# Attention q and k: six stacked copies stored, or three parts stored once and stacked by the loads

## The chip, the cores and the metric

The kernel runs on one core of one Trainium2 chip. The metric is the device time of one execution in microseconds (us); several executions are timed and their median is given. A profile is one further execution, recorded by the hardware profiler.

## The reference

A network of sixteen layers over x of 4 x 1024 tokens with 128 channels: attentions, feed-forward layers, state-space layers. Every layer adds its output to x. Five of them (2, 4, 6, 8 and 14) are causal attentions with 16 heads; cut to what matters, as layer 4 has it:

```python
def proj(w, b):
    y = jnp.einsum('bsd,ed->bse', x, w) + b
    return y.reshape(B, S, N_HEADS, HEAD_DIM).transpose(0, 2, 1, 3)
q = rope(proj(wq, bq))
k = rope(proj(wk, bk))
v = proj(wv, bv)
score = jnp.einsum('bhqd,bhkd->bhqk', q, k) / math.sqrt(HEAD_DIM)
score = jnp.where(causal[None, None], score, -jnp.inf)
attn = jax.nn.softmax(score, axis=-1)
out = jnp.einsum('bhqk,bhkd->bhqd', attn, v)
```

Layers 4 and 6 have rope (a rotation of channel pairs by position), layer 2 weights the probabilities by a decay instead, layer 8 has biases and no rope, layer 14 has heads of 4 channels and a bias by distance (alibi). The others have heads of 8 channels.

## The kernel before, in words

x stays in SBUF as 128 channels x 4096 tokens. Each attention is a layer norm, a projection stage (`attn_project`) and a core stage (`attn_core`); between stages all engines meet at a barrier.

**Projection.** The tokens are taken in eight halves of 512, two per batch element (here: batch). For q and for k TensorE multiplies, VectorE writes the value to t1 (with rope three operations), and three bf16 parts are made: ScalarE casts the value to the high part, GpSimd subtracts, ScalarE casts the rest to the middle part, and VectorE (plain layers) or GpSimd (rope) subtracts again for the low part. hi, mid and low count 16 of these each, four per batch. The parts lie in the SBUF tensor `part`, 128 channel rows (64 in layer 14).

A score product in near-f32 precision is six products of parts, `PAIRS`. They are summed in the contraction of one matmul: a head's q has 6 slots of dq rows, slot s holding part PAIRS[s][0], and its k the same with PAIRS[s][1]. SyncE (L506 to L518) waits for a batch's parts and stores the six q slots to DRAM, each a transfer of 128 rows of 1024 tokens; ScalarE stores the six k slots between its casts (`store_k`, L616). After batch 0's twelve stores have landed, SyncE loads stacks 0, 1 and 2. The stage ends when all stores have landed.

**A stack** is four heads: two (i) in partitions 0 and 64 onwards, two (p) side by side in the row. `load_stack` (L438) fills it by four transfers of 48 rows x 2 pieces of 1024, and two small ones of zero rows; layer 14 adds two of alibi rows. Three buffers take turns. Rows r0 to r0 + 2 of q hold the negated row maxima, in three parts as well.

**Core.** Sixteen groups, one per stack. In group n TensorE works through a string `PLAN` of a (scores for the row maxima, of the stack ahead), b (scores for the exponential, of stack n) and v (values). VectorE reduces the a scores (L1046); unit a number 14 of a group (16 in layer 2) is the first to read stack n + 2, and waits for its load (`stack_in`). SyncE's order in group n is: the maxima's rows of stack n + 1 (`max_rows`, L746), then, when all b scores of stack n are done, the load of stack n + 3, then every fourth group a step of the batch that is finished (`sums_back` L761, `inverse_rows` L765, `heads_back` L768), then the group's output and sums (L752, L754).

```python
if n + 1 < GROUPS:
    max_rows(n + 1)
if n + 3 < GROUPS:
    sp.wait_ge(b_ready, 4 * NS_ * (n + 1))
    load_stack(sp, n + 3)
...
if n >= 4 and n % 4 == 0:
    sums_back(n // 4 - 1, HEADS)
```

Of the kernel before, what the change touches and what calls it, by code (L numbers as in the profile page):

```python
# [10 lines left out]
BF16 = mybir.dt.bfloat16  # L11
# [5 lines left out]
P = 128  # L17
# [386 lines left out]
PAIRS = ((0, 0), (0, 1), (0, 2), (1, 0), (1, 1), (2, 0))  # L404
# [12 lines left out]
def attention(net, tag, w, dq, scale, rope=False, alibi=False, decay=False, bias=False, out_bias=False):  # L417
# [4 lines left out]
    parts = {n: nc.dram_tensor(f"{tag}_{n}_rows", (B * HEADS * 6 * dq, S), BF16, kind="Internal").ap() for n in "qk"}  # L422
# [3 lines left out]
    with stage(nc, tag) as (sb, ps, sem):  # L426
# [11 lines left out]
        def load_stack(sp, n):  # L438
            u = n % 3
            for n_, dst in (("q", qs[u]), ("k", ks[u])):  # L440
                src = parts[n_][n * 24 * dq:(n + 1) * 24 * dq, :].rearrange("(p i r) t -> i r p t", p=2, i=2)
                for i in range(2):
                    sp.dma_start(dst[64 * i:64 * i + 6 * dq, :, :], src[i]).then_inc(stack_in[u], 16)
# [28 lines left out]
def attn_project(net, tag, w, dq, rope, bias, decay, parts, v, qs, ks, load_stack, load_consts_):  # L472
# [4 lines left out]
    with stage(nc, tag + "_proj") as (sb, ps, sem):  # L477
# [22 lines left out]
        with nc.Block() as block:  # L500
            @block.sync
            def _(sp):
# [3 lines left out]
                for b in range(B):  # L506
                    sp.wait_ge(hi, 4 * (b + 1))
                    sp.wait_ge(mid, 4 * (b + 1))
                    sp.wait_ge(low, 4 * (b + 1))
                    for slot in range(6):  # L510
                        sp.dma_start(parts["q"].rearrange("(b h s d) t -> b s h d t", b=B, s=6, d=dq)[b, slot],
                                     part[0:R, 0, PAIRS[slot][0], b * S:(b + 1) * S]
                                     ).then_inc(stored if b else first_stored, 16)
                    if b == 0:
                        sp.wait_ge(first_stored, 16 * 12)
                        for n in range(3):
                            load_stack(sp, n)
# [84 lines left out]
            def _(act):  # L602
# [13 lines left out]
                def store_k(b):  # L616
                    act.wait_ge(low, 4 * b + 4)
                    for slot in range(6):
                        act.dma_start(parts["k"].rearrange("(b h s d) t -> b s h d t", b=B, s=6, d=dq)[b, slot],
                                      part[0:R, 1, PAIRS[slot][1], b * S:(b + 1) * S]  # L620
                                      ).then_inc(stored if b else first_stored, 16)
# [44 lines left out]
def attn_core(net, tag, w, dq, r0, scale, alibi, decay, out_bias, v, qs, ks, heads_out, sums, rsums, consts, c_in,  # L666
# [36 lines left out]
    with stage(nc, tag + "_core") as (sb, ps, sem):  # L703
# [2042 lines left out]
```

## Time and profile before

| | |
|---|---|
| median of 3 runs | 5800.48 us (5797.83 to 5809.48) |
| the profiled execution's own time | 5776.4 us |
| its span, first to last instruction | 5774.7 us |
| busy: TensorE, VectorE, ScalarE, GpSimd | 4735.2, 3787.2, 3161.8, 1684.7 us |
| mean granted TensorE clock | 0.919 of full speed |
| moved by DMA | 239.83 MB in 146884 packets |

The span is cut into instructions with start, length and what ended the idle time before them. Engines: PE is TensorE, DVE VectorE, ACT ScalarE, POOL GpSimd, SP SyncE; a q behind the name (SPq, ACTq) marks the issuing of a transfer, whose length is the time that the engine's queue is held. A packet is one contiguous piece that a DMA engine moves. A window's row gives the stretch, its length, the busy time (and count) of PE, PEld, DVE, ACT and POOL, the granted clock, the mean busy share of the 16 DMA engines and GB/s. "l_" in a name stands for any layer.

### The profile page before, as it was taken

The numbers are of one execution on the slowest core, as the hardware profiler recorded it, in microseconds if no ns is written. First come the engines' busy times: TensorE is split into PE (matmuls) and PEld (weight loads), VectorE is DVE, ScalarE is ACT, GpSimd is POOL, SyncE is SP. The second block draws the span as 40 slices with busy tenths as digits, with TensorE's granted clock in tenths as the row PEclk, the third lists the DMA queues.
The fourth block names the chain that finished last, engine by engine and source line by source line (L and its number), as shares of the span: only waits on it lengthen the run. The fifth ranks groups of instructions, "written<-read, shape, count | busy, mean of one in ns | idle before, by whom it ended". The sixth has DMA issues, their size and how long they took to land. (4 is left out here: it accounts for less than half of the span.)

```text
span 5774.7 us, 90836 instructions
## 1 busy us (share of the span) xinstructions
PE 4735.2 (82%) x33596; PEld 2081.6 (36%) x33596; DVE 3787.2 (66%) x4596; ACT 3161.8 (55%) x6002; POOL 1684.7 (29%) x1468
## 2 busy tenths in 40 slices
PE   5677667998569977699776998589867799699999
PEld 2233224443223336233352333256422344233344
DVE  6899658886579943799437992677539710699410
ACT  5655444766438853388534885444466421388621
POOL 0666315886032225323152220000006400222100
PEclk8899888999779989799897999789989999799999
DMA  0000012221032225322253220000000000211100
GB/s 27 0 1 1 4 49 76 44 44 29 10 112 42 55 65 177 115 51 51 74 154 120 50 46 20 6 10 2 5 10 0 20 0 0 60 31 45 42 0 15
DMA packets 146884, 239.83 MB, mean 42 GB/s; under 512 B 37382, under 2 KB 66930, under 8 KB 145076
## 3 DMA queue, kind: packets, MB, share of 16 engines
q1 hardware_dynamic: 125748, 197.74, 12.8%
q10 hardware_dynamic: 15744, 28.32, 1.5%
q0 software_dynamic: 4992, 8.41, 0.6%
q8 instruction: 254, 4.16, 0.3%
q14 instruction: 146, 1.20, 0.1%
HBM read 153.93 MB, written 80.31 MB: 41 GB/s over the span
## 5 line engine op out<-in xcount | busy, mean ns | idle before, releaser
L946 ACT ACTIVATE l_core_probs<-l_core_ps_scores_b 128x512 f32<-128x512 f32 (+3 forms) x3840 | 1611.3, 510 | 570.7 <-PE l_core_ps_scores_b L862 415.6
L1046 DVE TENSOR_REDUCE l_core_chunk_max<-l_core_ps_scores_a 128x2 f32<-128x1024 f32 (+3 forms) x1280 | 1253.3, 1020 | 83.9 <-PE l_core_ps_scores_a L847 48.6
L862 PE MATMUL l_core_ps_scores_b<-l_q_rows_sb,l_k_rows_sb 64*128 64x512 bf16 (+3 forms) x3840 | 944.5, 333 | 32.2 <-ACT l_core_probs L946 9.7
L847 PE MATMUL l_core_ps_scores_a<-l_k_rows_sb,l_q_rows_sb 64*128 64x512 bf16 (+3 forms) x3840 | 740.2, 346 | 121.1 <-DVE l_core_chunk_max L1046 44.7
L995 POOL TENSOR_SCALAR_AFFINE_SELECT l_core_probs<-l_core_probs 128x512 f32<-128x512 f32 x512 | 325.4, 636 | 1161.4 <-ACT l_core_probs L946 1156.4
L877 PE MATMUL l_core_ps_acc<-l_core_probs,l_v 128*9 128x512 f32 (+3 forms) x6144 | 647.7, 494 | 16.0 <-ACT l_core_out_sums L928 9.0
L862 PEld LDWEIGHTS l_core_ps_scores_b<-l_q_rows_sb,l_k_rows_sb 64*128 64x128 bf16 x3840 | 304.0, 94 | 690.0 <-ACT l_core_probs L946 607.9
L1046 DVE TENSOR_REDUCE l_core_neg_max<-l_core_ps_scores_a 128x2 f32<-128x256 f32 (+3 forms) x640 | 493.4, 819 | 84.8 <-PE l_core_ps_scores_a L807 83.0
L1917 POOL TENSOR_TENSOR l_scan_bx<-l_xs,l_scan_b_rows 128x1024 f32<-128x1024 f32 x192 | 452.3, 2356 | 224.2 <-DVE l_scan_states L1927 217.8
L1927 DVE TENSOR_TENSOR_SCAN l_scan_states<-l_scan_ps_decay,l_scan_bx 128x1024 f32<-128x1024 f32 x192 | 439.7, 2290 | 40.8 <-POOL l_scan_bx L1917 15.3
L965 POOL TENSOR_TENSOR l_core_probs_decayed<-l_core_probs,l_decay 128x1536 f32<-128x1536 f32 (+2 forms) x160 | 394.0, 2487 | 142.9 <-ACT l_core_probs L946 142.9
L807 PE MATMUL l_core_ps_scores_a<-l_mask_q_rows,l_identity_halves 64*128 64x128 bf16 (+1 forms) x5120 | 402.9, 211 | 0.0
L1862 PE MATMUL l_scan_ps_y<-l_scan_states_c,ident 128*128 128x512 f32 x768 | 362.5, 595 | 0.0
L1890 ACT ACTIVATE l_scan_ps_decay<-l_delta,l_a_cols 128x1024 f32<-128x1024 f32 x192 | 214.6, 1118 | 253.3 <-DVE l_scan_states L1927 253.3
L847 PEld LDWEIGHTS l_core_ps_scores_a<-l_k_rows_sb,l_q_rows_sb 64*128 64x128 bf16 x3840 | 204.0, 94 | 371.8 <-DVE l_core_chunk_max L1046 174.6
L807 PEld LDWEIGHTS l_core_ps_scores_a<-l_mask_q_rows,l_identity_halves 64*128 64x128 bf16 x5120 | 305.5, 98 | 79.0 <-issue 15.3
L1561 DVE SCALAR_TENSOR_TENSOR x_res<-l_ps_out,l_scales,x_res 128x512 f32 x16 | 12.0, 751 | 486.9 <-PE l_ps_out L1534 486.9
L1550 ACT ACTIVATE l_gelu<-l_ps_hidden,l_scales 128x512 f32<-128x512 f32 x128 | 87.9, 687 | 384.7 <-PE l_ps_hidden L1522 384.7
L1812 POOL TENSOR_TENSOR l_xs<-l_xs,l_delta x16 | 28.9, 1805 | 776.3 <-DVE l_delta L1802 776.3
L1852 PE MATMUL l_scan_ps_c_rows<-l_bc_parts,l_spread 128*128 128x512 bf16 x384 | 117.9, 389 | 148.2 <-DVE l_scan_states_c L1935 148.2
L638 POOL MEMSET l_q_rows_sb<- 128x2048 bf16 x5 | 9.0, 1804 | 764.8 <-POOLq L49 764.8
L1935 DVE TENSOR_TENSOR l_scan_states_c<-l_scan_states,l_scan_ps_c_rows 128x1024 f32<-128x1024 f32 x192 | 229.4, 1195 | 1.4 <-PE l_scan_ps_c_rows L1852 1.4
(323 smaller groups left out, 7711.9 us busy)
## 6 DMA issues: line engine op xcount, KB each, us to landing
l_slots_weights<-m_both_dram SPq DMA_DIRECT2D x78, 512.0 KB, 4.7
l_k_rows<-l_proj_parts ACTq DMA_DIRECT2D x96, 256.0 KB, 5.3
l_q_rows<-l_proj_parts SPq DMA_DIRECT2D x96, 256.0 KB, 5.1
l_q_rows_sb<-l_q_rows SPq DMA_DIRECT2D x128, 192.0 KB
l_k_rows_sb<-l_k_rows SPq DMA_DIRECT2D x128, 192.0 KB
l_heads_out<-l_core_out_sums SPq DMA_DIRECT2D x300, 32.0 KB
l_core_heads<-l_heads_out SPq DMA_DIRECT2D x15, 512.0 KB, 5.6
l_core_inverse_rows<-l_rsums SPq DMA_DIRECT2D x15, 512.0 KB, 7.0
```

What stands on the lines that cost most here:

```text
L807: mm = nc.tensor.matmul(dst[:, cols[h]], eye[rows, h, :], mask[rows, h, cols[h]], start=False, stop=(h == 1))
L847: mm = nc.tensor.matmul(slot[:, i, 0:w], qs[n % 3][rows, p, qt * P:(qt + 1) * P], ks[n % 3][rows, p, c * NT:c * NT + w], start=True, stop= ...
L862: mm = nc.tensor.matmul(pb[m % 3][:, 0:w], ks[n % 3][rows, p, kt * P:(kt + 1) * P], qs[n % 3][rows, p, q0:q0 + w], start=True, stop=not diag)
L877: mm = nc.tensor.matmul(acc[32 * j:32 * j + 9, NT - w:NT], ones9[:, :] if decay else v[:, n, kt, j, :], pt[:, ts % RP, j, 0:w], start=(kt ...
L946: nc.scalar.activation(pt[:, ts % RP, j, 0:w], pb[m % 3][:, 0:w], ACT.Exp, scale=scale).then_inc(b_free, 1)
L965: nc.gpsimd.tensor_tensor(pw[:, had_decay(ts) % RW, :, 0:wd], pt[:, ts % RP, :, 0:wd], dtab[:, :, off:off + wd].to_broadcast((P, 4, wd)), ...
L995: nc.gpsimd.affine_select(block_, block_, [[0, 4], [1, P]], ALU.is_ge, none, base=0, channel_multiplier=-1).then_inc(cut, 1)
L1046: nc.vector.tensor_reduce(to, pa[e % 2][:, :, 0:width_a(qt, c)], AX.X, ALU.max, negate=True).then_inc(a_free, 1)
L1862: mm = nc.tensor.matmul(acc[:, c * NT:(c + 1) * NT], net.ident[:, :], hc[:, q % R, c * NT:(c + 1) * NT], start=(n == 0), stop=(n == NS - 1))
L1917: nc.gpsimd.tensor_tensor(bx[:, q % R, :], xs[:, h, b * S:(b + 1) * S], bs[:, q % RS, :], ALU.mult).then_inc(bx_done, 1)
L1927: nc.vector.tensor_tensor_scan(hs[:, q % RS, :], pa[:, :], bx[:, q % R, :], 0.0, ALU.mult, ALU.add).then_inc(scanned, 1)
L1935: nc.vector.tensor_tensor(hc[:, q % R, :], hs[:, q % RS, :], pc[:, :], ALU.mult).then_inc(hc_done, 1)
```

## The change

DRAM holds each of the three parts of q and of k once. SyncE stores them, all six, after every half of a batch, in transfers of 128 rows of 512 tokens; ScalarE stores nothing. `load_stack` puts the six slots together: `RUNS` lists runs of slots that share one part of q (a broadcast source) and take successive parts of k. The host permutes the columns of the q and k weights, biases and rope tables so that the rows which lie side by side in a stack are neighbours in DRAM; it costs the device nothing. Stack 0 is loaded after batch 1's stores, stack 1 after batch 2's, stack 2 at the start of the core. `sums_back` stands ahead of the load of a stack.

```diff
-PAIRS = ((0, 0), (0, 1), (0, 2), (1, 0), (1, 1), (2, 0))
+RUNS = ((0, 0, 0, 3), (3, 1, 0, 2), (5, 2, 0, 1))
...
-    parts = {n: nc.dram_tensor(f"{tag}_{n}_rows", (B * HEADS * 6 * dq, S), BF16, kind="Internal").ap() for n in "qk"}
+    parts = {n: nc.dram_tensor(f"{tag}_{n}_rows", (3, B * HEADS * dq, S), BF16, kind="Internal").ap() for n in "qk"}
...
-            for n_, dst in (("q", qs[u]), ("k", ks[u])):
-                src = parts[n_][n * 24 * dq:(n + 1) * 24 * dq, :].rearrange("(p i r) t -> i r p t", p=2, i=2)
-                for i in range(2):
-                    sp.dma_start(dst[64 * i:64 * i + 6 * dq, :, :], src[i]).then_inc(stack_in[u], 16)
+            for i in range(2):
+                lines = slice(n * 4 * dq + i * 2 * dq, n * 4 * dq + (i + 1) * 2 * dq)
+                for at, part, first, slots in RUNS:
+                    rows = slice(64 * i + at * dq, 64 * i + (at + slots) * dq)
+                    src = parts["q"][part, lines, :].rearrange("(o d p) t -> o d (p t)", o=1, p=2)
+                    sp.dma_start(qs[u][rows, :, :].rearrange("r p t -> r (p t)"),
+                                 src.to_broadcast((slots, dq, 2 * S))).then_inc(stack_in[u], 16)
+                    src = parts["k"][first:first + slots, lines, :].rearrange("s (d p) t -> s d (p t)", p=2)
+                    sp.dma_start(ks[u][rows, :, :].rearrange("r p t -> r (p t)"), src).then_inc(stack_in[u], 16)
...
-                    for slot in range(6):
-                        sp.dma_start(parts["q"].rearrange("(b h s d) t -> b s h d t", b=B, s=6, d=dq)[b, slot],
-                                     part[0:R, 0, PAIRS[slot][0], b * S:(b + 1) * S]
-                                     ).then_inc(stored if b else first_stored, 16)
-                    if b == 0:
+                    for h in range(2):
+                        sp.wait_ge(hi, 4 * b + 2 * h + 2)
+                        sp.wait_ge(mid, 4 * b + 2 * h + 2)
+                        sp.wait_ge(low, 4 * b + 2 * h + 2)
+                        for j, n in enumerate("qk"):
+                            for s_ in range(3):
+                                sp.dma_start(parts[n][s_, b * R:(b + 1) * R, h * NT:(h + 1) * NT],
+                                             part[0:R, j, s_, b * S + h * NT:b * S + (h + 1) * NT]
+                                             ).then_inc(stored if b else first_stored, 16)
+                    if b == 1:
                         sp.wait_ge(first_stored, 16 * 12)
-                        for n in range(3):
-                            load_stack(sp, n)
+                    if b in (1, 2):
+                        load_stack(sp, b - 1)
...
-                def store_k(b):
...
-        NST = 16 * (6 + (2 if alibi else 0))
+        NST = 16 * (14 + (2 if alibi else 0))
...
+                load_stack(sp, 2)
                 max_rows(0)
                 for n in range(GROUPS):
                     if n + 1 < GROUPS:
                         max_rows(n + 1)
+                    if n >= 4 and n % 4 == 0:
+                        sums_back(n // 4 - 1, HEADS)
                     if n + 3 < GROUPS:
                         sp.wait_ge(b_ready, 4 * NS_ * (n + 1))
                         load_stack(sp, n + 3)
...
-                    if n >= 4 and n % 4 == 0:
-                        sums_back(n // 4 - 1, HEADS)
```

How the order on the engines moves. SyncE's queue in the projection of layer 2, before: the q stores of batch 0, three stacks, the q stores of batches 1 to 3 (l_q_rows and l_k_rows are the DRAM tensors, the same with _sb the stack buffers; the shape is that of the transfer's destination or source rows).

```order
L511 DMA l_q_rows<-l_proj_parts 16x8x1024 x6
L443 DMA l_q_rows_sb<-l_q_rows 48x2x1024 x2
L443 DMA l_k_rows_sb<-l_k_rows 48x2x1024 x2
L445 DMA l_q_rows_sb<-zero_rows_dram 3x2048 x2
L443 DMA l_q_rows_sb<-l_q_rows 48x2x1024 x2
```

The same queue now, from the last half of batch 1 to the middle of stack 0.

```order
L521 DMA l_q_rows<-l_proj_parts 128x512 x3
L521 DMA l_k_rows<-l_proj_parts 128x512 x3
L448 DMA l_q_rows_sb<-l_q_rows 24x1x2048
L451 DMA l_k_rows_sb<-l_k_rows 24x1x2048
L448 DMA l_q_rows_sb<-l_q_rows 16x1x2048
L451 DMA l_k_rows_sb<-l_k_rows 16x1x2048
L448 DMA l_q_rows_sb<-l_q_rows 8x2048
L451 DMA l_k_rows_sb<-l_k_rows 8x2048
```

A store is one transfer of 128 rows of 512; the four large loads of a stack have become twelve, of 24, 16 and 8 rows, and stores of the batches 2 and 3 stand behind one stack each.

ScalarE's queue at the end of batch 1 of layer 2, before, with the six k stores between the casts.

```order
L613 ACTIVATE l_proj_parts<-l_proj_t 128x512 x2
L607 ACTIVATE l_proj_parts<-l_proj_t 128x512 x2
L613 ACTIVATE l_proj_parts<-l_proj_t 128x512
L619 DMA l_k_rows<-l_proj_parts 16x8x1024 x6
L607 ACTIVATE l_proj_parts<-l_proj_t 128x512
```

The same place now.

```order
L623 ACTIVATE l_proj_parts<-l_proj_t 128x512 x2
L617 ACTIVATE l_proj_parts<-l_proj_t 128x512 x2
L623 ACTIVATE l_proj_parts<-l_proj_t 128x512
L617 ACTIVATE l_proj_parts<-l_proj_t 128x512
L623 ACTIVATE l_proj_parts<-l_proj_t 128x512
```

The casts follow one another, and the queue holds no transfer.

SyncE's queue in the core of layer 2 at n = 4, before.

```order
L746 DMA l_q_rows_sb<-l_core_max_parts 2x16x128 x3
L443 DMA l_q_rows_sb<-l_q_rows 48x2x1024 x2
L443 DMA l_k_rows_sb<-l_k_rows 48x2x1024 x2
L445 DMA l_q_rows_sb<-zero_rows_dram 3x2048 x2
L761 DMA l_core_inverse<-l_sums 128x128
```

And now.

```order
L746 DMA l_q_rows_sb<-l_core_max_parts 2x16x128 x3
L761 DMA l_core_inverse<-l_sums 128x128
L448 DMA l_q_rows_sb<-l_q_rows 24x1x2048
L451 DMA l_k_rows_sb<-l_k_rows 24x1x2048
L448 DMA l_q_rows_sb<-l_q_rows 16x1x2048
```

The fetch of the sums has moved from behind the load to ahead of it.

## Rows read from the trace of the kernel before

**Rows 1.** The page, part 1: busy time, share of the span and instructions of each engine.

```profile
PE 4735.2 (82%) x33596; PEld 2081.6 (36%) x33596; DVE 3787.2 (66%) x4596; ACT 3161.8 (55%) x6002; POOL 1684.7 (29%) x1468
```

**Rows 2.** Timeline of SyncE, layer 2's projection: start, length, engine, line, what, count.

```profile
844.14 6.92 SPq L511 DMA_DIRECT2D l_q_rows<-l_proj_parts  x6
855.20 0.82 SPq L443 DMA_DIRECT2D l_q_rows_sb<-l_q_rows  x2
866.51 21.31 SPq L511 DMA_DIRECT2D l_q_rows<-l_proj_parts  x18
```

**Rows 3.** Timeline of SyncE: a 128-row load of a weight, and alibi rows (layer 14).

```profile
808.18 0.43 SPq L137 DMA_DIRECT2D l_proj_w<-a_wk_dram  x1
...
4960.18 0.91 SPq L449 DMA_DIRECT2D l_q_rows_sb<-alibi_q_dram  x1
```

**Rows 4.** Timeline of ScalarE, layer 2's projection; in brackets the idle time before.

```profile
844.06 6.30 ACTq L619 DMA_DIRECT2D l_k_rows<-l_proj_parts  x6
850.40 0.63 ACT L607 ACTIVATE l_proj_parts<-l_proj_t 128x512 bf16<-128x512 f32 x1 [7.91 <-issue]
...
857.01 5.84 ACTq L619 DMA_DIRECT2D l_k_rows<-l_proj_parts  x6
```

**Rows 5.** Windows, first store to the core's first VectorE instruction; last: clock, DMA share, GB/s.

```profile
844.14:893.20 49.06, 24.40 (x80) 14.55 (x78) 25.58 (x54) 12.31 (x22) 13.56 (x10) 0.72 0.89 307
1612.34:1670.35 58.01, 30.48 (x100) 17.39 (x100) 32.93 (x63) 13.79 (x24) 29.19 (x24) 0.80 0.83 259
2324.53:2383.92 59.39, 30.23 (x100) 16.22 (x100) 31.42 (x64) 13.79 (x24) 29.30 (x24) 0.80 0.82 253
3034.83:3086.39 51.56, 23.50 (x79) 13.74 (x78) 25.88 (x53) 12.30 (x22) 13.56 (x10) 0.71 0.88 291
4949.21:4993.51 44.30, 21.80 (x79) 13.80 (x78) 25.46 (x54) 12.30 (x22) 13.53 (x10) 0.73 0.74 176
```

**Rows 6.** Timeline of VectorE, end of layer 2's projection and start of its core.

```profile
880.88 1.66 DVE L598 COPY l_v<-l_proj_ps_v 128x128 f32<-128x128 f32 x8
...
889.90 0.88 DVE L598 COPY l_v<-l_proj_ps_v 128x128 f32<-128x128 f32 x4 [0.16 <-PE l_proj_ps_v L532]
893.20 0.48 DVE L1004 MEMSET l_core_ps_acc<- 128x512 f32 x1 [2.42 <-PEq L49]
```

**Rows 7.** Timelines of SyncE and TensorE, layer 4's core: stack 3's load and first use.

```profile
1727.83 0.81 SPq L443 DMA_DIRECT2D l_q_rows_sb<-l_q_rows  x2
...
1743.15 0.22 PE L847 MATMUL l_core_ps_scores_a<-l_k_rows_sb,l_q_rows_sb 64*128 64x128 bf16 x2
```

**Rows 8.** Windows: 2 KB stores, 4 KB loads, 1 KB rows, a stack's load (2 KB).

```profile
846.00:849.50 3.50, 2.69 (x4) 0.50 (x2) 0.47 (x1) 0.00 (x0) 0.00 (x0) 0.67 1.03 370
1140.00:1141.00 1.00, 1.00 (x24) 0.79 (x22) 0.89 (x3) 0.89 (x4) 1.00 (x1) 1.00 1.05 389
3613.30:3614.30 1.00, 1.00 (x4) 0.50 (x3) 0.00 (x0) 0.52 (x2) 0.00 (x0) 1.00 0.56 152
984.00:989.00 5.00, 5.00 (x85) 2.38 (x82) 4.16 (x5) 3.82 (x9) 4.34 (x3) 1.00 0.81 162
```

**Rows 9.** Timeline of GpSimd, layer 4's projection.

```profile
1605.01 1.15 POOL L643 TENSOR_TENSOR l_proj_t<-l_proj_t,l_proj_parts 128x512 f32<-128x512 f32 x1 [0.33 <-ACT l_proj_parts L613]
1606.12 1.61 POOL L650 TENSOR_TENSOR l_proj_parts<-l_proj_t,l_proj_parts 128x512 f32 x1
```

**Rows 10.** DMA packets in 983:990 (stack load), 960.6:965 (output), 979:983.1 (maxima), 1399.5:1408 (heads, inverse).

```profile
DMA packets 461, 0.83 MB, mean 118 GB/s; under 512 B 70, under 2 KB 70, under 8 KB 460
...
DMA packets 74, 0.17 MB, mean 39 GB/s; under 512 B 36, under 2 KB 36, under 8 KB 72
...
DMA packets 102, 0.02 MB, mean 6 GB/s; under 512 B 102, under 2 KB 102, under 8 KB 102
...
DMA packets 192, 0.68 MB, mean 80 GB/s; under 512 B 28, under 2 KB 28, under 8 KB 191
```

**Rows 11.** Transfers by line, whole trace: a small one; last, us to landing.

```profile
l_rsums<-l_core_inverse SPq DMA_DIRECT2D x15, 64.0 KB, 2.1
```

More of the change, by code:

```diff
@@ L614, in second @@
                                          ACT.Copy).then_inc(mid, 1)
-                def store_k(b):
[L617 to L621, printed above, removed]
                 for b in range(B):
@@ L2572, in thirds, with stack_order @@
     return np.stack([hi, mid, low])
+def stack_order(dq):
+    return np.arange(HEADS * dq).reshape(4, 2, 2, dq).transpose(0, 2, 3, 1).reshape(-1)
 def shape_constants():
@@ L2582, in shape_constants @@
     freq = (1.0 / 10000.0 ** ((d // 2 * 2).astype(f) / 8)).astype(f)
-    theta = pos[None] * freq[:, None]
-    sign = np.where(d % 2 == 0, -1.0, 1.0).astype(f)[:, None]
+    order = stack_order(8)
+    theta = pos[None] * freq[order, None]
+    sign = np.where(d[order] % 2 == 0, -1.0, 1.0).astype(f)[:, None]
     rope = np.stack([np.cos(theta), np.sin(theta) * sign], 1).astype(f)
@@ L2626, in attention_layouts @@
     swap = np.arange(P) ^ 1
+    order, order4 = stack_order(8), np.tile(stack_order(4), 2)
     out = {}
     w = i["L0_attn_b_W_attn"]
-    out.update(a0_wq=w[:, :P], a0_wk=w[:, P:2 * P], a0_wv=w[:, 2 * P:], a0_wo=i["L0_attn_b_W_proj"])
+    out.update(a0_wq=w[:, :P][:, order], a0_wk=w[:, P:2 * P][:, order], a0_wv=w[:, 2 * P:], a0_wo=i["L0_attn_b_W_proj"])
     for n, wn, f in (("a1", "L1_attn_a_w", lambda m: m.T), ("b1", "L1_attn_b_W", lambda m: m)):
         q, k, bq, bk = f(i[wn + "q"]), f(i[wn + "k"]), i[wn[:-1] + "bq"], i[wn[:-1] + "bk"]
-        out.update({f"{n}_wq": q, f"{n}_wk": k, f"{n}_wv": f(i[wn + "v"]), f"{n}_wo": f(i[wn + "o"]),
-                    f"{n}_wq_sw": q[:, swap], f"{n}_wk_sw": k[:, swap], f"{n}_bq": one(bq), f"{n}_bk": one(bk),
-                    f"{n}_bq_sw": one(bq[swap]), f"{n}_bk_sw": one(bk[swap]),
+        out.update({f"{n}_wq": q[:, order], f"{n}_wk": k[:, order], f"{n}_wv": f(i[wn + "v"]), f"{n}_wo": f(i[wn + "o"]),
+                    f"{n}_wq_sw": q[:, swap[order]], f"{n}_wk_sw": k[:, swap[order]],
+                    f"{n}_bq": one(bq[order]), f"{n}_bk": one(bk[order]),
+                    f"{n}_bq_sw": one(bq[swap[order]]), f"{n}_bk_sw": one(bk[swap[order]]),
                     f"{n}_bv": row(i[wn[:-1] + "bv"]), f"{n}_bo": one(i[wn[:-1] + "bo"])})
@@ L2638, in attention_layouts @@
     for j, n in enumerate("qkv"):
-        out[f"a2_w{n}"] = w[:, :, j].reshape(D, P)
-        out[f"a2_b{n}"] = (row if n == "v" else one)(b[:, j].reshape(P))
+        cols = slice(None) if n == "v" else order
+        out[f"a2_w{n}"] = w[:, :, j].reshape(D, P)[:, cols]
+        out[f"a2_b{n}"] = (row if n == "v" else one)(b[:, j].reshape(P)[cols])
     out.update(a2_wo=i["L2_attn_a_out_W"], a2_bo=one(i["L2_attn_a_out_b"]))
-    out.update(b3_wq=np.tile(i["L3_attn_b_Wq"], (1, 2)), b3_wk=np.tile(i["L3_attn_b_Wk"], (1, 8)),
+    out.update(b3_wq=i["L3_attn_b_Wq"][:, order4], b3_wk=np.tile(i["L3_attn_b_Wk"], (1, 8))[:, order4],
                b3_wv=np.tile(i["L3_attn_b_Wv"], (1, 4)), b3_wo=i["L3_attn_b_Wp"], b3_bo=one(i["L3_attn_b_bp"]))
```

6 lines of the change are left out of this document (removed).

## The prediction

> **What bounds the kernel now.** First the page's busy times [rows 1]: no engine is busy throughout (TensorE 82% of the span), so the answer lies in stages. The edit touches the five attentions in two places: the projection stage, which writes q and k to DRAM, and the core, which reads them back as stacks.
>
> In the projection the queues of SyncE and ScalarE come first. In layer 2 SyncE takes 6.92 us to issue six q stores and 21.31 us for the other eighteen [rows 2]: 1.15 and 1.18 us each, while a plain 128-row transfer is issued in 0.43 us [rows 3]. ScalarE spends 6.30 us issuing six k stores and stands 7.91 us without a cast [rows 4]. The windows say why: from the first store to the first instruction of the core the DMA engines are 89% busy at 307 GB/s in layer 2, 82 to 88% in layers 4, 6 and 8, and 74% in layer 14, over 49.06, 58.01, 59.39, 51.56 and 44.30 us [rows 5]. The stage is nearly bound by the transfers. VectorE's last copy of v ends at 890.78 and the core begins at 893.20 [rows 6], so compute, delayed by the blocked ScalarE, ends only just before the transfers.
>
> In the core a stack's load starts when the group before has done its matmuls, 1727.83 in layer 4, and TensorE first reads that stack at 1743.15 [rows 7]: 15.3 us of room. The same distance holds in layers 6, 8 and 14; layer 2 has more. Thirteen stacks of each attention are loaded so.
>
> **The change, part by part.**
>
> *Stores.* 24 q stores on SyncE and 24 k stores on ScalarE, 256 KB each, become 48 stores of 128 KB on SyncE: the bytes halve, their 1 KB rows are as many as the 2 KB rows were. A full-rate window of 2 KB stores gives 16 x 2048 / 370 = 89 ns per row and engine, and a 1 KB one 0.56 x 16 x 1024 / 152 = 60 ns [rows 8]. The ends are 45 (half of 89) and 89 ns; I take 60, the row of that size. A store is then 8 rows on each of 16 engines, 0.48 us, and its issue 0.43 us plus a gap of some 0.04 [rows 3]. Twelve stores, a batch's worth, cost 5.7 us either way, where 12 old ones took 12 x 8 x 89 ns = 8.5 us of transfer. Issue bounds: 0.43 as here, or 1.15 as the old stores [rows 2]; I take 0.43, since the old ones were held up by the full DMA engines.
>
> *ScalarE without stores.* It loses the 6 us stalls. Its casts of a batch take 6.61 us (850.40 to 857.01) [rows 4]; in the layers with rope GpSimd sets the pace, 1.15 + 1.61 + 0.33 = 3.1 us per half of q or k, 12.3 per batch [rows 9]. Compute then ends about 20 us after the first store in the plain layers (30 with v's copies, 9.9 us from 880.88 by the same copies) and 37 us in the rope ones. That is ahead of what follows, so the casts hide behind the transfers and are costed at nothing.
>
> *Loads of a stack.* Four transfers of 192 KB become twelve: for q and for k and for each half of the partitions, runs of three, two and one slots, of 24, 16 and 8 rows of 4 KB. The bytes are the same, the engines are not. The trace tells how many engines a transfer uses, since each engine adds one packet of under 512 B to the data: four old loads and two of three rows leave 70 = 4 x 16 + 2 x 3; eight stores of 8 and 1 rows leave 36 = 4 x 8 + 4 x 1; three transfers whose destination has an outer dimension of 2 leave 102 - 96 = 6 [rows 10]. The source counts too: a load of 96 rows and one whose destination has 96 rows but whose source repeats 12 leave 28 = 16 + 12 [rows 10]. In the new loads the source's outer dimension is the slot, 3 or 2, so I forecast 3, 2 and 8 engines. The Trainium skill has this as a rule (DMA: Bandwidth & Descriptors, "Rules for kernel authors": an outermost dimension of c copies keeps the whole transfer on at most c engines), and it speaks against this edit; by that rule, the trace agrees.
>
> The first two engines then carry 8 + 8 + 1 rows, four times over: 68 rows of 4 KB per stack, 272 KB, where each of 16 carried 48 KB. A stream of 4 KB rows gives 16 x 4096 / 389 = 168 ns [rows 8], so a stack takes 11.4 us. Bounds: 68 x 120 = 8 us if twice the 1 KB price is all that 4 KB needs, and 68 x 328 = 22 us at twice the 164 ns which 2 KB rows took when 16 engines wrote 48 partitions [rows 8]. I take 168, same size and direction; with two or three engines at work there is less to collide than in that window. A layer-14 stack has half the rows: 34 and one or two more, 6.1 us, about what its sixteen issues cost, two of them 0.91 us [rows 3].
>
> *In the core.* 11.4 us plus the 2.1 us that a small transfer needs from issue to landing [rows 11] is 13.5 us, within 15.3. Costed at nothing, with 1.8 us of cover left. SyncE issues 14 instead of 6 transfers, some 5 us; the sums' stores behind them are not needed for a group's length. Moving the sums' fetch ahead of the load takes it out from behind those long transfers; its one reader, VectorE's inversion, comes within the same group after a third of its work, so it gains nothing. Stack 2 now loads at the start of the core and is needed a group and a half later: hidden. The maxima's rows of stack 0, queued behind it, exist only when all 24 of its reductions are done: hidden too.
>
> *The projection's new length.* Stacks 0 and 1 are loaded between stores, so each of the first two engines does, after batch 1's last stores: load, 12 stores, load, 12 stores = 2 x (11.4 + 5.7) = 34.2 us. Before it: batch 1's casts, 6.6 us after batch 0's (12.3 with rope), and six stores, 2.9 us. After it: 2.1 us to land and the 2.4 us between 890.78 and 893.20 [rows 6]. Together 48.2 us plain, 53.9 with rope, and 6.6 + 2.9 + 2 x (6.1 + 5.7) + 4.5 = 37.6 in layer 14. Against rows 5:
>
> - layer 2: 49.06 to 48.2, -0.9
> - layer 4: 58.01 to 53.9, -4.1
> - layer 6: 59.39 to 53.9, -5.5
> - layer 8: 51.56 to 48.2, -3.4
> - layer 14: 44.30 to 37.6, -6.7
>
> The sum is -20.6 us, 0.36%. The profiled execution took 5776.4 us, 24 below the median of the runs, 5800.5; I subtract the difference from the median: **5780 us**. What comes next as the bound in the projection is the pair of engines that load the stacks, with the other fourteen idle for two thirds of that time.
>
> **The rivals.**
>
> *A: the loads spread over more engines,* or the pair is faster than I think. Then SyncE's issue is the limit: 14 issues at 0.3 to 0.43, 5.6 us, in place of 11.4, twice, so another 11.6 us off in each of four layers and none in layer 14, where issue already counts: -67, 5734 us. For it: halved bytes, a queue that is freed of backlog. Against: the packet counts [rows 10]. 0.12.
>
> *B: slower, a stack that comes late in the core.* Its place is TensorE's first read of a stack in layers 4, 6 and 8, 13 times each. It decides from 68x + 2.1 > 15.3, x = 194 ns per row. At 220 ns, a third more than my row and well below the 328 of the bound, each stack comes 1.8 us late: 39 x 1.8 = 68 us, and each load in the projection is 3.5 us longer, 2 x 4 x 3.5 = 28. With -20.6 that is +76, 5876 us; at 205 ns it is 29 + 20 - 20.6 = +28, 5829 us. For it: rows of 164 ns per 2 KB in this very load [rows 8]. Against: these came when 16 engines wrote to a few partitions. 0.15.
>
> *C: hardly any change, SyncE alone is the bound.* If a store costs 0.6 us to issue rather than 0.47, twelve take 7.2 us: 2 x 1.5 + 0.8 = 3.8 us more in each of five layers, and the sum is -1.6: 5799 us. At 0.78 it would be about +26. For it: all 48 stores now stand in one queue behind 28 loads, with ScalarE's queue empty. The Trainium skill says that issuing from more engines saves only the sequencer's time (DMA: Bandwidth & Descriptors, "Rules for kernel authors"). 0.2.
>
> **How the numbers follow.** The forecast has 0.53: -11 to -36 us for 4 KB rows between 177 and 150 ns and stores between 0.5 and 0.43 us. A measurement of this kernel tells 0.2%, about 12 us, from no change. Faster: A whole, and four fifths of the forecast, 0.55. Slower: B, and of C the part with dearer issue, 0.15 + 0.06 = 0.21. The rest, 0.24, is within. The range leaves out half of A below (5746) and the worse half of B above (5825).
>
> **What would show it.** Right: packets under 512 B of a stack load at 3, 2 and 8 per transfer; a stack's 4 KB packets over some 11 to 12 us; no wait of TensorE for a stack; stages between 48 and 54 us; ScalarE without gaps for stores. Wrong: rows of a "DMA q_rows_sb" releaser before TensorE's score matmuls in layers 4, 6 and 8 (B); store issues above 0.55 us with idle DMA engines (C); a projection under 45 us (A). The forecast falls altogether if the core's groups change in length at all.

## The result, and the profile after

The change measures **5795.89 us** against 5804.11 us for the kernel before (21 runs each): a ratio of 0.9987, 95% interval 0.9981 to 0.9993. A second set of runs gave 0.9991 (0.9982 to 1.0000). That is 8 us less, two fifths of the 20.6 us that the prediction forecast, and within the 0.2% that it called no change. The bytes written to DRAM fell by a third (80.31 to 52.00 MB), DMA packets by a tenth, and almost nothing came of it.

The page of the kernel after, parts 1 to 3; TensorE's busy time is as in [rows 1].

```profile
PE 4718.3 (81%) x33501; PEld 2088.3 (36%) x33596; DVE 3782.7 (65%) x4596; ACT 3159.8 (55%) x6002; POOL 1685.3 (29%) x1468
...
DMA packets 132106, 211.55 MB, mean 37 GB/s; under 512 B 36422, under 2 KB 93619, under 8 KB 130293
...
HBM read 153.93 MB, written 52.00 MB: 36 GB/s over the span
```

The windows of the kernel after, from the first store to the core's first VectorE instruction, answer to [rows 5].

```profile
838.79:888.65 49.86, 21.79 (x84) 12.84 (x82) 27.71 (x57) 14.31 (x26) 15.61 (x12) 0.76 0.46 159
1603.24:1657.77 54.53, 30.42 (x107) 16.14 (x105) 37.61 (x68) 15.09 (x27) 34.74 (x27) 0.90 0.44 145
2326.83:2381.75 54.92, 31.42 (x107) 17.34 (x105) 38.21 (x69) 15.10 (x27) 34.72 (x27) 0.89 0.43 144
3049.63:3099.13 49.50, 20.89 (x83) 12.84 (x82) 27.95 (x57) 14.23 (x25) 15.55 (x12) 0.81 0.48 160
4965.35:5018.48 53.13, 21.88 (x83) 13.06 (x82) 27.37 (x57) 14.08 (x25) 15.56 (x12) 0.75 0.33 79
```

The DMA engines went from 0.74 to 0.89 busy to under half, and yet four windows lie within 1.7 us of the forecast 48.2 and 53.9; the fifth, layer 14, took 53.1 where 37.6 was forecast. A window starts at its first store, though, which now leaves after half a batch and not a whole one. So the fair measure is a whole stage, from VectorE's clearing of v's last column (L549; L539 before) to its clearing of the accumulator (L1005; L1004), and from there to the next stage's first matmul. Read from the two traces, in us (the first pair of columns is the projection stage, the last the core):

| layer | projection before | after | forecast change | change | core before | after | change |
|---|---|---|---|---|---|---|---|
| 2 | 65.87 | 62.79 | -0.9 | -3.1 | 532.07 | 532.00 | -0.1 |
| 4 | 78.48 | 70.49 | -4.1 | -8.0 | 437.68 | 442.93 | +5.3 |
| 6 | 79.85 | 70.89 | -5.5 | -9.0 | 437.42 | 441.27 | +3.9 |
| 8 | 68.48 | 62.20 | -3.4 | -6.3 | 437.95 | 442.28 | +4.3 |
| 14 | 60.91 | 66.00 | -6.7 | +5.1 | 440.13 | 437.55 | -2.6 |
| sum | | | -20.6 | -21.3 | | | +10.8 |

So the projections gave what was forecast, by accident: four gave twice as much, layer 14 took 5.1 us in place of giving 6.7. And half of it was lost again in the cores.

Two things in this table and this profile are not the change's. Layer 14's core is 2.6 us shorter because TensorE was busy 2.6 us less with the same matmuls; its granted clock was 0.94 before and 0.95 after. Windows of that core, before and after:

```profile
4993.51:5433.64 440.13, 406.78 (x4136) 145.38 (x4137) 369.55 (x434) 334.52 (x806) 110.06 (x198) 0.94 0.12 32
5018.48:5456.03 437.55, 404.14 (x4136) 145.72 (x4137) 369.44 (x434) 334.16 (x806) 110.93 (x198) 0.95 0.13 34
```

In all the profiles the cores of layers 4 to 14 that wait neither for a stack nor for the sums take between 436.8 and 440.4 us, so a difference of 3 us in one core of one profile says nothing by itself. And the expert stages (layers 5 and 7) took 210 and 214 us in the profile shown, against 196 and 197 before; a second profile of the same kernel, run e11, shows 199 and 194. That is the spread of single executions.

**The pair of engines.** Timeline of SyncE, kernel after, layer 2 (start, length, what):

```profile
842.93 1.29 SPq L521 DMA_DIRECT2D l_q_rows<-l_proj_parts  x3
...
851.76 1.47 SPq L521 DMA_DIRECT2D l_k_rows<-l_proj_parts  x3
853.27 0.85 SPq L448 DMA_DIRECT2D l_q_rows_sb<-l_q_rows  x1
854.17 0.72 SPq L451 DMA_DIRECT2D l_k_rows_sb<-l_k_rows  x1
854.94 0.64 SPq L448 DMA_DIRECT2D l_q_rows_sb<-l_q_rows  x1
...
860.74 0.58 SPq L453 DMA_DIRECT2D l_q_rows_sb<-zero_rows_dram  x2
861.44 1.33 SPq L521 DMA_DIRECT2D l_q_rows<-l_proj_parts  x3
...
880.47 1.45 SPq L521 DMA_DIRECT2D l_k_rows<-l_proj_parts  x3
```

Three windows after its last issue (881.92), with nothing but DMA in them:

```profile
881.94:883.44 1.50, 0.00 (x0) 0.00 (x0) 0.00 (x0) 0.00 (x0) 0.00 (x0) 0.50 0.59 206
883.44:887.14 3.70, 0.00 (x0) 0.00 (x0) 0.00 (x0) 0.00 (x0) 0.00 (x0) 0.50 0.12 43
887.14:888.65 1.51, 0.00 (x0) 0.00 (x0) 0.00 (x0) 0.18 (x1) 0.00 (x0) 0.50 0.00 1
```

A load takes 8 us to issue (14 transfers), not 5. Still the queue is not what ends the stage: 6.7 us pass between its last issue and the core, and for 3.7 of them the DMA share is 0.12, two engines of sixteen (0.12 x 16 = 1.9), working off the stores' 1 KB rows that stand behind the loads. The trace does not name the engines; that they are the pair of the prediction is what run e1 shows.

**Layer 14.** Timeline of SyncE, same kernel:

```profile
4965.35 1.79 SPq L521 DMA_DIRECT2D l_q_rows<-l_proj_parts  x3
4967.19 1.88 SPq L521 DMA_DIRECT2D l_k_rows<-l_proj_parts  x3
...
4978.77 1.88 SPq L521 DMA_DIRECT2D l_k_rows<-l_proj_parts  x3
4980.68 0.79 SPq L448 DMA_DIRECT2D l_q_rows_sb<-l_q_rows  x1
...
4989.80 0.82 SPq L457 DMA_DIRECT2D l_q_rows_sb<-alibi_q_dram  x1
4990.74 1.78 SPq L521 DMA_DIRECT2D l_q_rows<-l_proj_parts  x3
...
5014.05 1.87 SPq L521 DMA_DIRECT2D l_k_rows<-l_proj_parts  x3
```

There is no gap above 0.2 us in 50.6 us. A store of 64 rows takes 0.6 us to issue, more than one of 128 rows (0.44 above), and a load 10 us, while the DMA share of this stage is 0.33. Here SyncE alone is the bound: rival C, in one layer.

**The core.** The page of waits, kernel after, has a row that the kernel before has not (us in total, times, longest):

```profile
PE l_core_ps_scores_a L848 <- DMA l_q_rows_sb<-zero_rows_dram: 8.6, 6, 2.1
```

These six waits are at stacks 9 and 13 of layers 4, 6 and 8; all others still come in time. In layer 4, stack 9 was issued from 1862.37 on and TensorE stood at 1878; windows of that load:

```profile
1866.37:1868.37 2.00, 1.95 (x21) 0.66 (x20) 1.87 (x3) 1.39 (x5) 0.64 (x1) 1.00 0.25 82
1868.37:1870.37 2.00, 2.00 (x28) 0.70 (x29) 1.86 (x2) 1.49 (x6) 1.02 (x2) 1.00 0.27 90
1870.37:1872.37 2.00, 1.90 (x22) 0.73 (x20) 2.00 (x3) 2.00 (x5) 0.26 (x1) 1.00 0.61 152
1872.37:1874.37 2.00, 1.90 (x21) 0.70 (x20) 2.00 (x3) 2.00 (x6) 0.00 (x0) 1.00 1.07 272
1874.37:1876.37 2.00, 1.83 (x18) 0.56 (x17) 1.79 (x3) 1.93 (x5) 0.00 (x0) 1.00 0.89 164
1876.37:1878.37 2.00, 1.47 (x11) 0.21 (x10) 1.39 (x2) 1.76 (x5) 0.00 (x0) 1.00 0.24 92
```

and what SyncE issued behind it:

```profile
1870.34 0.36 SPq L768 DMA_DIRECT2D l_core_heads<-l_heads_out  x1
1870.74 0.58 SPq L771 DMA_DIRECT2D l_core_inverse_rows<-l_rsums  x1
```

The heads come back, two transfers of 512 KB, just where the load is in its second half. The median 4 KB packet that starts between 1862.37 and 1878, the heads' own among them, takes 211 ns; in the load before (stack 8) it was 159.

The six waits are 8.6 us, where the three cores are 13.5 us longer. TensorE was also busy 4.1 us longer in them for the same matmuls. In the second profile (e11) the same six waits are 10.3 us and the busy time is 1.4 us longer, at cores 13.0 us longer.

### The profile page after: what moved, and what is told of

The parts are those of the page before. It is cut to its first block and busy times, and to the rows that moved or that the text cites. A ratio compares the mean times of both kernels' runs of the same rounds, so it can differ in the third digit from the quotient of the medians.

```text
span 5794.8 us, 91401 instructions
## 1 busy us (share of the span) xinstructions
PE 4718.3 (81%) x33501; PEld 2088.3 (36%) x33596; DVE 3782.7 (65%) x4596; ACT 3159.8 (55%) x6002; POOL 1685.3 (29%) x1468
```

## The experiments

Theory P: the pair of engines ends four projections and makes stacks 9 and 13 late. Theory S: SyncE's queue does. Twelve runs follow. Each ratio is to the kernel before in the same set, where it took 5772 to 5776 us and not 5804: compare the ratios, not the times. The change itself stands at 0.9987. "Stage" below is as in the table above, read from one profile of each run, and "us below the change" is the difference of two ratios.

**e1, loads over eight engines.** In the stack's rows d comes first and the slot second, for q and k alike:

```diff
-src = parts["q"][part, lines, :].rearrange("(o d p) t -> o d (p t)", o=1, p=2)
-... src.to_broadcast((slots, dq, 2 * S))
+src = parts["q"][part, lines, :].rearrange("(d o p) t -> d o (p t)", o=1, p=2)
+... src.to_broadcast((dq, slots, 2 * S))
-src = parts["k"][...].rearrange("s (d p) t -> s d (p t)", p=2)
+src = parts["k"][...].rearrange("s (d p) t -> d s (p t)", p=2)
```

> The rows of a stack are ordered d first and slot second within each of the three runs, so that each load has 8 (layer 14: 4) rows as its slowest dimension and not 3 or 2; q and k keep the same order, nothing else changes. Theory P (the first two engines, which carry 68 of the 4 KB rows of a load, bound the projections of layers 2, 4, 6 and 8, and slow the loads at stacks 9 and 13): 24 rows on each of 8 engines, 24 x 159 ns = 3.8 us in place of 10.8 us; the projections of layers 2 to 8 end 2 to 4 us sooner (until SyncE's own issue is the bound: its last store was issued 5 us before the packets ended), 8 to 14 us in all; TensorE's waits on the stack load at stacks 9 and 13 go, 4 us a layer, 12 us in all; layer 14 unchanged. Sum: 5770 to 5780 us against 5796. Rival S (SyncE's issue alone is the bound everywhere): projections unchanged, only the core waits may shrink, above 5785 us. Rival D (the time is set by all the DMA engines' total bytes): no change, 5796 us.

Measured: 5726.04 us, 0.9921 (0.9907 to 0.9935), 38 us below the change. Windows of layers 2 and 14:

```profile
840.20:885.03 44.83, 21.80 (x84) 12.89 (x82) 27.72 (x58) 14.31 (x26) 15.60 (x12) 0.79 0.52 177
...
4895.11:4947.74 52.63, 21.90 (x83) 13.09 (x82) 27.36 (x58) 14.08 (x25) 15.56 (x12) 0.75 0.33 80
```

The projections of layers 2 to 8 are 5.2, 5.0, 4.9 and 4.5 us shorter, layer 14's is not (65.5); the row of waits for a stack is gone and the cores of layers 4, 6 and 8 are back at 437.6, 438.6 and 437.8. Same bytes, same number of transfers, same issue time (7.5 us busy per load): only the engines differ. P holds. The gain was to be 16 to 26 us and is 38: the four projections gave 20 where 8 to 14 were expected, and the five attentions' stages account for 32 by one profile of each. The Trainium skill has the remedy (DMA: Bandwidth & Descriptors, "Rules for kernel authors"): put outermost a dimension whose size is a multiple of 16. Only 8 rows (4 in layer 14) were to be had here, and that step in its direction was worth 38 us.

**e2 and e6, the heads fetched earlier.** e2 puts the fetch ahead of the load in the same pass; e6 one pass earlier, behind the output's stores (the edit of e6):

```diff
-                    if n >= 4 and n % 4 == 2:
-                        heads_back(n // 4 - 1, HEADS)
                     if n < GROUPS - 1:
                         output(n)
+                    if n >= 4 and n % 4 == 1:
+                        heads_back(n // 4 - 1, HEADS)
```

> In the core SyncE issues the fetch of the heads (two transfers of 512 KB) before it waits for the stack's buffer, no longer behind the load of the stack at n = 6, 10 and 14. Theory P (the load of stacks 9 and 13 is late because those 512 KB transfers run beside it): the waits of TensorE on the stack load in layers 4, 6 and 8 go, cores of 441 to 443 us become about 438, some 4 us a layer: 12 us less, 5784 us. Rival W (the load is late for another reason, e.g. its 14 issues on SyncE): the waits stay, 5796 us.

Measured: 5754.05 us, 0.9966 (0.9952 to 0.9979). The time came out as expected, but not the waits:

```profile
PE l_core_ps_scores_a L848 <- DMA l_q_rows_sb<-zero_rows_dram: 5.7, 6, 1.9
```

In e2 the fetch stands behind the maxima's rows, so it was issued at 1860.01, 1.5 us before the load (1861.51), and ran beside it all the same. So e6:

> The fetch of the heads is issued one unit earlier than in the run e2, behind the output stores of n = 5, 9, 13, some 13 us ahead of the load of stacks 9 and 13 (in e2 it was issued 1.5 us ahead of the load, because it stood behind the max rows, and half of the waits stayed). Theory H (the 1 MB of the heads beside the load is what makes stacks 9 and 13 late): the waits of TensorE on the stack load are gone in all three layers, cores of layers 4, 6, 8 at 437.5 to 438.5 us, about 12 us less than the change: 0.9966 of before. Rival W (stacks 9 and 13 are late by their place, not by the heads): waits stay, 0.9987.

Measured: 5750.54 us, 0.9955 (0.9942 to 0.9969). The heads' fetch is issued at 1853.59 in layer 4, 13.3 us ahead of the load (1866.88), and of the row of waits one of 0.3 us is left. Theory H holds: same pair, same load, no collision, no wait. The cores of layers 4, 6 and 8 took 439.7, 440.3 and 437.3 where 437.5 to 438.5 was expected: in the first two TensorE was busy 405.8 and 405.9 us with the same matmuls, against 403.6 and 403.7 in the kernel before, so these 2 us are no wait for a stack.

**e3, layer 14's k parts stored by ScalarE** (`"q" if dq == 4 else "qk"` on SyncE, and three k stores on ScalarE half a batch behind its casts):

> Layer 14 alone: the k parts are stored by ScalarE's queue, one half batch behind its casts, q parts and loads stay on SyncE. Theory S14 (SyncE's issue bounds layer 14's projection: 48 stores of 64 rows at 0.62 us and two loads at 10 us): 24 stores fewer, 24 x 0.62 = 15 us off SyncE's queue, of which about 10 us until the casts and the pair of engines bound: projection of layer 14 from 66.0 to 54 to 58 us, total 5784 to 5788 us. Rival P14 (the DMA engines bound it): within 1 us of 5796.

Measured: 5753.84 us, 0.9963 (0.9949 to 0.9977). Layer 14's window:

```profile
4932.60:4976.29 43.69, 21.35 (x84) 12.21 (x82) 28.67 (x57) 14.29 (x26) 15.70 (x12) 0.80 0.40 97
```

The timeline of SyncE there, six stores of q, the last that it issues in the stage, where twelve stood before:

```profile
4970.04 3.70 SPq L521 DMA_DIRECT2D l_q_rows<-l_proj_parts  x6
```

43.7 us where it was 53.1, and the stage 56.3 where it was 66.0; the other projections did not move. S14 holds.

**e4, stores of whole batches** (six of 2 KB rows per batch, not twelve of 1 KB):

> Parts are stored once per batch (6 transfers of rows of 2 KB) and no longer per half batch (12 of 1 KB); all else as in the change, which stands at 0.9987 of the kernel before. Theory S14 (layer 14's projection is bound by SyncE's issue, 0.62 us a store whatever its bytes): 24 issues fewer there, 15 us of queue, of which 8 to 10 us show until the casts bound: 66.0 becomes 56 to 58 us. Theory P (the pair of engines bounds layers 2 to 8): 2 KB packets take a little less than two of 1 KB, so 1 to 2 us a layer, less where the last batch's stores now begin later. Sum about 0.9963 of before. Rival B (a store's issue grows with its bytes, or the coarser stores delay the chain): 0.9987 or above.

Measured: 5756.78 us, 0.9970 (0.9960 to 0.9979). Layer 14's stage is 58.3, the others are 0.2 to 1 us shorter than the change's. Three of its layer-14 stores, timeline of SyncE:

```profile
4971.35 1.79 SPq L520 DMA_DIRECT2D l_q_rows<-l_proj_parts  x3
```

A store of twice the bytes takes the same time to issue. S14 holds from the other side. The halves, which brought the first store 4 us forward, gain nothing in layer 2: its stage is 61.8 without them.

**e5, stacks 0 and 1 loaded behind all stores:**

> Stacks 0 and 1 are loaded after all stores, not between the stores of batches 1, 2 and 3; parts are still stored once and stack 2 still loads in the core. Theory P: the pair of engines has the same work but starts it later: the last store is issued about 16 us sooner in layers 2 to 8 only where the casts allow it (casts end 20 us before the last store's issue in layer 2), the loads then run as 2 x 11 us at the end of the queue with nothing beside them; total DMA work on the pair is the same, so the projections change by under 2 us each where the pair was never idle in between; I expect within 5 us of 5796. Rival O (the placement between the stores is what the gain comes from): each projection 8 to 16 us longer, 5836 to 5876 us.

Measured: 5764.27 us, 0.9986 (0.9977 to 0.9995), the same as the change. But the stages differ: 57.8 and 58.1 in layers 2 and 8 (4 to 5 us shorter), 75.8 and 76.7 in layers 4 and 6 (5 to 6 longer). By these stages it is better to store first where the casts are done early, and where rope makes them late, a load between fills the time. My claim of under 2 us in each was wrong; that the total came out as expected was luck.

**e9, the sums fetched behind the load again:**

```diff
-                    if n >= 4 and n % 4 == 0:
-                        sums_back(n // 4 - 1, HEADS)
                     if n + 3 < GROUPS:
                         sp.wait_ge(b_ready, 4 * NS_ * (n + 1))
                         load_stack(sp, n + 3)
...
+                    if n >= 4 and n % 4 == 0:
+                        sums_back(n // 4 - 1, HEADS)
```

> Only the place of the fetch of the sums is undone: behind the load of the stack again, as in the kernel before. It carries 64 KB a batch and VectorE inverts them two stacks later, so both theories say no change that can be measured (0.9987 +- 0.0005 of before). Rival Q: behind the load's 14 issues it waits for the pair of engines, the inverse comes late and TensorE waits on it: above 0.9995.

Measured: **5839.8 us, 1.0112** (1.0097 to 1.0127), 72 us above the change. It was the rival that came. "Two stacks later" had been read from no trace: in the change the inversion follows the sums' fetch by 11.7 us (1811.91 to 1823.58 below). Layer 4 of e9, timeline of SyncE:

```profile
1817.93 0.72 SPq L448 DMA_DIRECT2D l_q_rows_sb<-l_q_rows  x1
...
1825.27 0.59 SPq L453 DMA_DIRECT2D l_q_rows_sb<-zero_rows_dram  x2
1825.97 0.36 SPq L761 DMA_DIRECT2D l_core_inverse<-l_sums  x1
```

and of VectorE, with the idle time before the inversion in brackets:

```profile
1832.65 0.95 DVE L1010 RECIPROCAL l_core_inverse<-l_core_inverse 128x128 f32<-128x128 f32 x1 [4.39 <-DMA l_core_inverse<-l_sums]
```

and its rows of waits, of VectorE on the sums, and of TensorE on VectorE behind it (45.1 in the change):

```profile
DVE l_core_inverse L1010 <- DMA l_core_inverse<-l_sums: 51.3, 13, 5.3
PE l_core_ps_scores_a L848 <- DVE l_core_chunk_max L1047: 92.6, 76, 6.1
```

The sums are issued 8.0 us behind the load's first transfer, and their 128 packets of 512 B need until 1832.09, because they queue behind the load's rows (e13 will show this). The kernel before had 4.2 us to spare (last packet 1831.18, inversion at 1835.41): its load was issued in 2.4 us. The change has 10, by its timelines of SyncE and then of VectorE (last packet 1813.38):

```profile
1811.91 0.36 SPq L761 DMA_DIRECT2D l_core_inverse<-l_sums  x1
```

```profile
1823.58 0.94 DVE L1010 RECIPROCAL l_core_inverse<-l_core_inverse 128x128 f32<-128x128 f32 x1
```

Twelve of the thirteen waits are of this kind, three in each of layers 4, 6, 8 and 14 (the last one is in every profile). A stack with such a wait starts 6 to 7.5 us later than without in layers 4 to 8, and 3 to 5 in layer 14. So the third part of the change, a moved line, is what keeps the first from costing 1%.

**e13, e1 with the sums behind the load:**

> e1 (loads over 8 engines) with the sums fetched behind the load of the stack, as in e9. Theory Q (in e9 the sums' packets stood 5 us behind the load's on the pair of engines: issued at 1825.97, last packet at 1832.09): with the load spread the sums land about 2 us after their issue, VectorE waits 0 to 0.5 us: 0.992, e1's ratio. Rival I (the 14 issues on SyncE, 7.5 us, are what makes the sums late): the loss of e9 comes back whole, 60 us: 1.003.

Measured: 5741.01 us, 0.9947 (0.9933 to 0.9960): so only 15 of the 72 us are lost this time. In layers 4 to 8 VectorE waited twice, 0.5 and 0.7 us: the sums' packets pass in 0.4 to 1.2 us, theory Q. (Layer 4's core took 442.6 where e1 has 437.6, but TensorE was busy 4.4 us longer there at a granted clock of 0.94, so most of that is not the sums'.) In layer 14 it waited three times, 1.3 to 1.9 us, as in e9, and the core took 449.2 where e1 has 437.6:

```profile
5115.21 0.95 DVE L1010 RECIPROCAL l_core_inverse<-l_core_inverse 128x128 f32<-128x128 f32 x1 [1.25 <-DMA l_core_inverse<-l_sums]
```

There the 16 issues of a load (10 us) are what delays the sums: rival I, in that layer.

**e10, the first part of the change alone** (parts stored once, 14 transfers a load; stores, place of the loads and of the sums as before):

> The first part of the change alone: each part of q and k stored once and stacks put together by 14 transfers; everything else as in the kernel before (stores of whole batches, k by ScalarE, three stacks loaded straight behind batch 0's stores, the sums fetched behind the load of a stack). Theory Q (the sums, queued behind a load on the pair of engines, come 5 us late to VectorE 12 times; seen in e9) says: the projections gain some 20 us together, the waits at the sums cost 60 to 65 and those at stacks 9 and 13 12: 1.006 to 1.012 of before, slower. Rival: the stores' bytes are what counts and e9's loss came from something else in it: 0.996 to 0.999.

Measured: **5858.16 us, 1.0149** (1.0135 to 1.0163), beyond the 1.012 that I expected at most. The cores lose 78 us against the kernel before, as said. But the projections gain nothing: 72.8, 75.1, 75.7, 72.1 and 61.4 are 3.5 us more in all. In layer 2 SyncE stands in three loads on one pair of engines from 848.25 to 879.86, and its other nine stores come behind. So with a load on two engines its place between the stores seems to matter; this part of e10 was only read from its trace, not tried by itself.

**e7 and e12, towards a better version.** e7: e1, k parts stored by ScalarE in all layers, heads early. e12: the same with stores of whole batches.

> e1 (loads spread over 8 engines) with the k parts stored by ScalarE's queue in all five layers, and the heads fetched early as in e6. Theory S (once the pair is relieved SyncE's issue bounds all projections: in e1 its last store was issued 2.5 us before the core began): 24 issues x 0.45 = 11 us leave SyncE's queue; projections of layers 2 and 8 go from 57.6 to about 49 (VectorE's last copy of v then bounds), of 4 and 6 from 65.7 to 57 to 60, of 14 from 65.5 to 54 to 57. Sum 40 us below e1: 0.985 of before. Rival V (in e1 another engine had already taken over, or ScalarE's issues delay its casts by as much as they free SyncE): within 5 us of e1, 0.992.

Measured: **5697.16 us, 0.9866** (0.9849 to 0.9883), the fastest of all. Windows of layers 2, 4 and 14:

```profile
838.72:876.77 38.05, 22.86 (x84) 12.89 (x82) 28.65 (x57) 14.20 (x26) 14.29 (x12) 0.80 0.63 209
1593.01:1638.72 45.71, 30.30 (x107) 16.15 (x105) 37.57 (x68) 15.09 (x27) 34.71 (x27) 0.96 0.53 174
...
4876.32:4919.60 43.28, 21.40 (x84) 12.24 (x82) 28.72 (x57) 14.33 (x26) 15.97 (x12) 0.81 0.41 98
```

Stages of 50.8, 61.7, 63.7, 51.7 and 55.8 us: against e1 some 7, 4, 2, 6 and 10 less, 29 in all (40 expected). With the pair relieved SyncE's queue was the bound, theory S. The heads' earlier fetch gave nothing on top: the five cores are 2285.6 us together, 2284.5 in e1.

> e7 with stores of whole batches (half as many issues on both queues, seen in e4 to cost the same 0.45 or 0.6 us each). Theory S (SyncE's queue still ends e7's projections, its last store 2.5 us before the core): 1 to 3 us less in each of layers 2, 8 and 14, none or 1 us more in 4 and 6, where the casts of the last batch now gate all its stores: 0.9855 of before, e7's being 0.9866. Rival V (VectorE's copies of v or the casts already end them): equal to e7.

Measured: 5705.57 us, 0.9886 (0.9871 to 0.9901). Not better: layer 14's stage is 1.3 us shorter, the others are between 0.3 shorter and 1.0 longer, and the intervals of e7 and e12 overlap. Rival V is nearer; which engine ends e7's projections was not tested.

**e11, the change again:**

> The changed kernel once more, unaltered, for a second profile: in the first one the two expert stages (layers 5 and 7) took 210 and 214 us where the kernel before showed 196 and 197. If these are the spread of single executions, they lie between 191 and 200 here and the ratio is 0.998 to 0.999 of before; if the change lengthens them they stay above 208.

Measured: 5766.43 us, 0.9991 (0.9982 to 1.0000). Stages 62.9, 70.4, 71.2, 62.5 and 66.2, cores 532.0, 443.2, 441.4, 441.5 and 437.1: the table above repeats to 0.8 us.

## Why the prediction was wrong

Forecast -20.6 us, measured -8.2. The cores, costed at nothing, took 10.8 us; in the projections two misses, one of each sign, cancelled.

**Right, and shown.** A load sits on 3, 2 or 8 engines. DMA packets in the window of layer 2's projection (838.79 to 888.65):

```profile
DMA packets 7428, 7.93 MB, mean 159 GB/s; under 512 B 886, under 2 KB 7030, under 8 KB 7426
```

Two loads on 4 x (3 + 2 + 8) + 6 = 58 engines each and 48 stores on 16 make 884 of the 886. Alone, a load's last packet ends 12.5 us after its first issue (stack 2 of layers 2 to 8), where 13.5 was forecast to its landing. And 24 rows of 4 KB on each of eight in place of 68 on the first two gave 5 us a projection (e1). "What comes next as the bound in the projection is the pair of engines": yes, in four layers. The store's 0.43 us to issue held there. Rival A was rightly given little.

**The four projections gave twice the forecast** (26.4 against 13.9 us): the step that failed is the sum of three terms, "Before it", the pair's 34.2 us and "After it". The packets of the trace give each. The forecast counts from the end of batch 0's casts, which is the first store of its second half (842.93 in layer 2). Layers 2, 4, 6 and 8, in us:

| term | forecast | measured | error, four layers |
|---|---|---|---|
| to stack 0's first 4 KB packet | 9.5 and 15.2 | 12.0, 16.4, 16.9, 12.0 | 7.8 too short |
| the pair: loads and stores, to the last packet | 34.2 | 32.4, 32.2, 32.1, 32.0 | 8.1 too long |
| from there to the core | 4.5 | 1.4, 1.4, 1.4, 1.4 | 12.3 too long |

The last term is the largest. It adds up the 2.1 us that a small transfer takes from issue to landing and the 2.4 us between VectorE's last copy and the core, but these ran side by side: in the kernel before, too, the last packet ended at 891.73, 1.5 us ahead of the core's first instruction. The first term left out the 1.6 us between a load's first issue and its first packet, and batch 1's casts took 7.5 us in layer 2 and not 6.6. In the pair's term 1 KB rows take 46 to 49 ns and not 60; 4 KB rows take 159 (median), near the 168, and there are 70 and not 68 of them a load, with the zero rows: 2 x 70 x 0.159 + 192 x 0.047 = 31.3 us, 0.7 to 1.1 below what was measured. So the pair as the bound was right, the times around it were not, and the three errors together are 12.6 us too long.

**Layer 14: the step that failed is "its issue 0.43 us plus a gap of some 0.04", carried over to stores of 64 rows.** They take 0.6. With a load of 10 us rather than the 6.1 "about what its sixteen issues cost", SyncE was busy without a gap: 48 x 0.62 + 2 x 10 = 50 us. From the first load to the last store's issue that is 35.2 us, where 2 x (6.1 + 5.7) = 23.6 was forecast: 11.6 of the 11.8 us between -6.7 and the measured +5.1. The prediction had the mechanism as rival C, but priced it at one figure for all layers. Moving 24 stores to ScalarE gave 10 us back (e3), and halving their number 8 (e4). The Trainium skill says that a second issuing engine saves only the sequencer's issue time (DMA: Bandwidth & Descriptors, "Rules for kernel authors"). The runs agree, but that time was the whole bound here: "only" was 10 us in layer 14 (e3).

**The core: the step that failed is "Costed at nothing, with 1.8 us of cover left".** For a load that runs alone it is true. Two loads in thirteen do not: the heads' 1 MB is issued right behind them, a transfer that was harmless while a load was over in 6 transfers on 16 engines. With 1.8 us of cover it makes TensorE wait, 1.0 to 2.1 us each time. The cores of three layers are 4 to 5 us longer, 13.5 against the projections' 21.3, of which the waits are 8.6; the waits go when the heads are moved (e6) or the load is spread (e1). It is the very sign with which the forecast "falls altogether". Rival B named the right place and the right row of waits, but asked for slower packets everywhere. A cover so thin had to be checked against every transfer in the queue behind it.

**The sums: the sentence "so it gains nothing" is wrong.** Against the kernel before it is true by coincidence, since neither has a wait at those twelve places. But the change's own loads use up the sums' cover of 4.2 us, and without the moved line it would have been slower by over 1% (e9, e10). I read the deadline loosely, "within the same group", and never compared it with a time.

**Luck.** The projections' -21.3 us beside the forecast -20.6 is a sum of four layers with twice the gain and a fifth with a loss.

**Open.** e1 gained 38 us where its stages show 32, and of the cores' 13.5 us those beyond the waits have no cause that a run shows.

## What to carry to other kernels

When a transfer is cut into pieces, cost three things apart: its bytes, its issues (by shape, in the queue that gives them), and how many engines its outermost dimension gives it. Here the bytes fell, but the issues rose and the engines became fewer, and the time hardly moved; with the long dimension outermost, the stores shared between two queues and the heads fetched earlier (e7) the same idea gave 77 us in all, where the change alone had given 8. If a load comes to use nearly all its cover, list what is queued behind it and beside it with the time at which each is needed: the loss shows up there first.

## What the runs showed of the hardware that was not expected

- The issue of a transfer went by its shape, not by its bytes: 0.43 to 0.46 us (median) for 128 rows of 1 KB and 0.43 to 0.61 for 128 of 2 KB (e4), 0.6 for 64 rows of either, 0.72 for 24 rows in three slots, 0.62 for 16 in two, 0.28 to 0.43 for 8. Spreading the same 24 rows over eight engines left it nearly as it was (0.67, e1).
- Two transfers of 512 KB, begun in the second half of a load on few engines, brought the DMA share to 1.07 for 2 us and made TensorE wait 1.0 to 2.7 us for that load (the change and e11); 128 packets of 512 B issued right behind such a load needed 6.1 us (e9) in place of 1.5, and 1.4 to 2.1 behind a load spread over eight (e13).
- The same core took 437.1 us with TensorE busy 403.7 at a granted clock of 0.95 (e12, layer 6), and 440.4 with TensorE busy 407.0 at 0.94 (e7, layer 6), with no wait for a stack in either.
